# The state-space stage's two ends: scales and statistics across the stage border, and the order of the last outputs and turns

## The chip, the cores and the metric

The kernel runs on one core of a Trainium2 chip. Its engines are TensorE (PE; PEld is its weight load), VectorE (DVE), ScalarE (ACT), GpSimd (POOL) and SyncE (SP, which here issues DMAs). Each executes its own list of instructions in order; they meet only at semaphores. The metric is the device time of one execution in microseconds (us), lower is better; the time of a kernel is the median of several executions.

## The reference, cut to what matters

The input `x` is 16 batches of 512 rows with 128 elements. Four blocks follow one another, each with a residual:

```
x = x + attn_a(layernorm(x))      # attention with a Gaussian kernel, 16 heads
x = x + ffn(layernorm(x))         # local attention, and attention over routed tokens
x = x + attn_b(layernorm(x))      # the state-space block
x = x + ffn(layernorm(x))         # the same ffn again
```

The state-space block, on batches of 1024 rows in the original and of 512 here, is

```
u = h * rsqrt(mean(h*h) + 1e-6) * norm_weight     # h = layernorm(x)
Bu = u @ B_bar.T                                  # complex, 32 states
xs = scan over the rows of each batch: s = Lam_bar * s + Bu
y = 2 * (re(xs) @ C_re.T - im(xs) @ C_im.T) + D * u
out = h + y                                       # and x = x + out
```

The ffn behind it starts with two norms of its input and with router scores, the products of the normalised rows with two routing tokens.

## The kernel before, in words

`x` stays in SBUF the whole time as 64 tiles of 128 rows by 128 elements, four tiles to a batch, eight to a pair of batches. The stages are the Gaussian attention, the ffn's local part (`stage_light`, tag f1), its routed part (`stage_heavy`, tag f1), the state-space stage (`stage_ssm`), and the ffn again with tag f2. Every stage is a block: all engines finish it before any engine starts the next. Inside a block the order of each engine is written out by hand and the engines wait for counts of semaphores. In these sections a stage's pairs are numbered 0 to 7.

**The routed stage**, `stage_heavy` (L1669), loops over n with steps of pair n, n-1 and n-2 interleaved. For the last pair (n = 8 and 9) there remain, on ACT, the exponentials, `turned(7)` (L1952, two copies out of PSUM, L1956) and `values(7)` (L1959); on PE `turn`, `values`, `output` and `scatter` (L1889); on DVE `places` (L2063), `nulls` (L2079), `heavy(7)` (L2085) and `residual(7)` (L2091, which adds the result to `x`). Behind each residual comes `statistics` (L2094): `bn_stats` of each of the pair's eight tiles and `bn_aggr`, giving mean and variance in `K["mv"]`. ACT's last instruction is a load of the table for square roots (L1988), which comes ahead of the stage that uses it.

**The state-space stage**, `stage_ssm` (L2142), starts with a chain on DVE over all 64 tiles (L2221 to L2233, each step waits for the one before): add 1e-5 to the variance, root (ACT, L2316), reciprocal, two products, add 1e-6, a second root (ACT, L2320), reciprocal, products. It yields four columns per tile: `a1`, `a0` (scale and bias of the doubly normalised row) and `h1`, `h0` (for x + layernorm(x)). PE turns the matrix `bb` (L2394) and ACT copies it (L2318). Then, per pair q:

- `rows(q)` on ACT (L2327) makes eight normalised tiles `un`; of pairs 0 and 1 ACT makes four tiles and DVE four (L2237).
- `turn(q)` on PE (L2403) transposes them into the two banks `tp`, and `leave(q)` on ACT (L2333) copies them out as `ut`.
- `inputs(q)` on PE (L2413), `rotate(q)` on DVE (L2244), a sum on POOL (L2388), `scan(q)` on DVE (L2249), `back(q)` on DVE (L2254).
- `outputs(q)` on PE (L2424, L2429) into the banks `yy`; it waits for `back(q)` and for DVE's `residual(q-1)`, which frees `yy`.
- `kept(q)` on POOL (L2380) puts h into `x`; `residual(q)` on DVE (L2261) adds `yy`; then `statistics(q)` (L2266, L2270), `root(q)` on ACT (L2337), `scales(q)` on DVE (L2277).
- `result(q)` on ACT (L2348) makes the normalised rows `y` of the next stage; of pair 7 it makes four tiles, DVE the other four (L2298).
- `turn_result(q, e)` on PE (L2440) transposes each half e of the pair into the one bank `ty`, `leave_result(q, e)` on ACT (L2342) copies it to `yt`, and `score(b)` on PE (L2446) multiplies it with the routing tokens into `srow`. At the very end DVE makes the columns `r2` and `rc` for the next stage with one more root (`two`, L2359), and ACT copies `srow` (L2370).

PE's loop (L2449) goes over p from -3 to 10 and in each round does `inputs(p+1)`, `turn_result(p-2, 0)`, `turn(p+2)`, `turn_result(p-2, 1)`, `outputs(p)` and, in odd rounds from 3 on, four scores. ACT's loop (L2352) has `rows(p+3)`, `leave_result(p-2, 0)`, `leave(p+2)`, `root(p-1)`, `leave_result(p-2, 1)`, `result(p-1)`. So the outputs of the last pair (p = 7) stand behind both turns of pair 5, and with one bank `ty` every turn waits for the copy of the turn before.

## Time and profile before

| | us |
|---|---|
| median of 3 runs | 1805.41 (1804.49 to 1809.51) |
| the profiled execution: its time | 1804.04 |
| the profiled execution: its span | 1802.2 |
| state-space stage in that span | 1084.6 to about 1185.3 |

The span runs from the first to the last instruction that the profiler recorded; the execution's time has some 2 us around it. The profile's mean granted clock of TensorE is 0.977 of full speed. In a timeline each row is one instruction, or several alike merged (x8), with its start, its length, the engine and the line, what it writes from what it reads, and in brackets how long the engine had been idle and whose instruction ended the wait. Ends of PE's matmuls are modelled, and merged matmuls overlap.

### The profile page before, as it was taken

To read this page: it belongs to the slowest core of one execution; us is meant where nothing else is said; L and a number is where in the kernel's file an instruction comes from. 1 tells how busy PE (TensorE), PEld (TensorE's weight loads), DVE (VectorE), ACT (ScalarE), POOL (GpSimd) and SP (SyncE) were. 2 spreads that over 40 slices of the span, in tenths; PEclk is the share of its full clock that TensorE was granted. 3 is DMA by queue.
4 is the path that set the end of the run, shared out by engine and by line. 5 is a ranking of instruction groups with operands and counts; after the bars stand their busy time and mean duration, and the time that the engine had idled before them with its cause. 6 is when DMAs were issued, how large, how long until landed. Compare 5 with 4: busy or idle time off the path is not lost. (4 is left out here: it accounts for less than half of the span.)

```text
span 1802.2 us, 68292 instructions
## 1 busy us (share of the span) xinstructions
PE 1646.6 (91%) x27609; PEld 1271.0 (71%) x27609; DVE 1458.1 (81%) x3482; ACT 1454.3 (81%) x4122; POOL 759.2 (42%) x853
## 2 busy tenths in 40 slices
PE   3888988898899999999997996879999999999897
PEld 1444444444588888888886874658888888888786
DVE  8999999999877777877898776747777777789775
ACT  4999999998788888888774666668888888877564
POOL 2010000001154554555446966425454545554795
PEclk7999999999999999999999998989999999999998
DMA  6656555552001010101012000000101010101211
GB/s 189 152 150 156 144 138 141 147 131 55 13 15 26 15 26 15 26 15 26 14 27 49 2 1 1 1 13 15 26 15 26 14 26 15 26 14 27 49 49 48
DMA packets 80041, 91.96 MB, mean 51 GB/s; under 512 B 11696, under 2 KB 67984, under 8 KB 79728
## 3 DMA queue, kind: packets, MB, share of 16 engines
q1 hardware_dynamic: 78432, 87.15, 19.3%
q8 instruction: 221, 3.62, 0.9%
q14 instruction: 92, 0.75, 0.1%
q10 hardware_dynamic: 1296, 0.44, 0.1%
HBM read 39.68 MB, written 31.10 MB: 39 GB/s over the span
## 5 line engine op out<-in xcount | busy, mean ns | idle before, releaser
L1633 POOL TENSOR_TENSOR f1l_pn<-f1l_p,f1l_rs 128x512 f32<-128x512 f32 (+1 forms) x256 | 206.3, 827 | 252.5 <-DVE f1l_rs L1326 250.4
L1633 POOL TENSOR_TENSOR f2l_pn<-f2l_p,f2l_rs 128x512 f32<-128x512 f32 (+1 forms) x256 | 206.2, 826 | 231.1 <-DVE f2l_rs L1326 231.1
L1205 ACT ACTIVATE f2l_p<-f2l_sm,f2l_nb 128x192 f32<-128x192 f32 x512 | 209.2, 435 | 43.0 <-DVE f2l_nb L1319 43.0
L1205 ACT ACTIVATE f1l_p<-f1l_sm,f1l_nb 128x192 f32<-128x192 f32 x512 | 209.4, 434 | 42.4 <-DVE f1l_nb L1319 37.8
L595 ACT ACTIVATE r_pr<-r_far 128x1536 f32<-128x1536 f32 x128 | 194.2, 1517 | 0.1
L432 PE MATMUL r_acc<-r_pr,r_vp 128*32 128x384 f32 x3528 | 189.6, 331 | 2.2 <-DVE r_pr L709 1.2
L698 DVE SCALAR_TENSOR_TENSOR r_pr<-r_pr,k_lo,r_cap 128x512 f32<-128x512 f32 x256 | 182.3, 752 | 10.4 <-ACT r_pr L595 10.0
L709 DVE TENSOR_SCALAR r_pr<-r_pr,k_hi,k_lo 128x768 f32<-128x768 f32 x256 | 164.1, 682 | 0.0
L595 ACT ACTIVATE r_pr<-r_near 128x1024 f32<-128x1024 f32 x128 | 138.4, 1082 | 2.8 <-PE r_near L403 2.8
L1319 DVE TENSOR_REDUCE f2l_nb<-f2l_sm 128x4 f32<-128x768 f32 x128 | 116.1, 948 | 15.8 <-PE f2l_sm L1019 15.8
L775 POOL TENSOR_TENSOR r_nw<-r_nv,r_nr 128x8 f32<-128x8 f32 x1 | 0.4, 356 | 295.1 <-ACT r_nr L570 295.1
L1319 DVE TENSOR_REDUCE f1l_nb<-f1l_sm 128x4 f32<-128x768 f32 x128 | 116.1, 948 | 8.4 <-PE f1l_sm L1019 8.3
L432 PEld LDWEIGHTS r_acc<-r_pr,r_vp 128*32 128x32 f32 x3528 | 85.8, 110 | 42.2 <-issue 29.6
L1342 DVE TENSOR_TENSOR f2l_ot<-f2l_xa,f2l_late 128x256 f32<-128x256 f32 x128 | 53.7, 419 | 75.7 <-ACT f2l_late L1197 75.7
L1205 ACT ACTIVATION_READ_ACCUMULATOR f2l_p<-f2l_sm,f2l_nb 128x1 f32 x512 | 113.0, 221 | 0.0
L1205 ACT ACTIVATION_READ_ACCUMULATOR f1l_p<-f1l_sm,f1l_nb 128x1 f32 x512 | 112.6, 220 | 0.0
L1332 DVE COPY f1l_pt<-f1l_tp 128x512 f32<-128x512 f32 x128 | 88.1, 688 | 21.8 <-PE f1l_tp L1038 18.9
L1332 DVE COPY f2l_pt<-f2l_tp 128x512 f32<-128x512 f32 x128 | 88.0, 688 | 18.7 <-PE f2l_tp L1038 15.4
L1342 DVE TENSOR_TENSOR f1l_ot<-f1l_xa,f1l_late 128x256 f32<-128x256 f32 x128 | 53.6, 419 | 61.0 <-ACT f1l_late L1197 60.8
L1019 PE MATMUL f2l_sm<-f2l_kt,f2l_qt 64*64 64x128 f32 (+1 forms) x3584 | 99.3, 248 | 0.4 <-ACT f2l_p L1205 0.4
L1019 PE MATMUL f1l_sm<-f1l_kt,f1l_qt 64*64 64x128 f32 (+1 forms) x3584 | 99.1, 248 | 0.0
L1019 PEld LDWEIGHTS f2l_sm<-f2l_kt,f2l_qt 64*64 64x64 f32 x3584 | 92.9, 134 | 0.8 <-ACT f2l_p L1205 0.6
(564 smaller groups left out, 5155.7 us busy)
## 6 DMA issues: line engine op xcount, KB each, us to landing
rbf_rows<-r_part SPq DMA_DIRECT2D x112, 128.0 KB, 2.1
r_qs<-rbf_rows SPq DMA_DIRECT2D x60, 192.0 KB
r_ks<-rbf_rows SPq DMA_DIRECT2D x60, 192.0 KB
f1l_vs<-f1l_vv SPq DMA_DIRECT2D x64, 128.0 KB, 2.5
f2l_vs<-f2l_vv SPq DMA_DIRECT2D x64, 128.0 KB, 2.4
rbf_rows<-r_part SPq DMA_DIRECT2D x16, 384.0 KB, 3.0
rbf_rows<-r_part SPq DMA_DIRECT2D x16, 256.0 KB, 3.0
out<-k_x SPq DMA_DIRECT2D x8, 512.0 KB, 3.2
```

What stands on the lines that cost most here:

```text
L432: mm = nc.tensor.matmul(acc[32 * g:32 * g + 32, q0:q0 + n], vp[:, par, t, g, 32 * q:32 * q + 32], pr[:, (PAIRS * b + 2 * q + g // 2) % RIN ...
L595: nc.scalar.activation(pr[:, n % RING, :, cols], src, ACT.Exp).then_inc(done, 1)
L698: ins = nc.vector.scalar_tensor_tensor(on, on, K["lo"][:, h:h + 1], cap[:, h, :].unsqueeze(1).broadcast_to([P, NT, P]), ALU.max, ALU.min)
L709: ins = nc.vector.tensor_scalar(off, off, hi, lo, ALU.min, ALU.max)
L775: nc.gpsimd.tensor_tensor(nw[:], nv[:], nr[:], ALU.mult).then_inc(s_nv, 1)
L1019: mm = nc.tensor.matmul(sm[64 * w:64 * w + 64, u % 2, e, cc * PW + P * side:cc * PW + P * side + kn], qt[r, par, c, at:at + W], kt[r, par, ...
L1205: ins = nc.scalar.activation(p[:, u % 2, k, :], sm[:, u % 2, k // 2, k % 2 * PW:(k % 2 + 1) * PW], ACT.Exp, bias=nb[:, u % 2, k:k + 1], ac ...
L1319: nc.vector.tensor_reduce(nb[:, u % 2, :], sm[:, u % 2, :, 0:2 * PW].rearrange("p a (k c) -> p a k c", k=2), AX, ALU.max, negate=True).the ...
L1332: nc.vector.tensor_copy(pt[:, u % 2, 0:HU * P], tp[:]).then_inc(s_pt, 1)
L1342: nc.vector.tensor_tensor(ot[:, u // 2 % 2, 2 * g:2 * g + 2, :], xa[:, 0, 0:2 * P].rearrange("p (c q) -> p c q", q=P), late[:, u % 2, :].r ...
L1633: ins = nc.gpsimd.tensor_tensor(pn[:, u % 2, at:at + HU * w].rearrange("p (k c) -> p k c", k=HU), p[:, u % 2, :, cols], r.broadcast_to([P, ...
```

## The change

Four things are done.

- The scales of pairs 0 to 6 (56 tiles) are made at the end of the f1 routed stage: `scales_begin` on DVE behind `nulls(7)`, `scales_end` on DVE between `heavy(7)` and `residual(7)`, their two roots on ACT as its last instructions. The load of the table for roots comes ahead of `turned(7)` for that. `a1`, `a0`, `h1`, `h0` become tensors that outlive the stage.
- The statistics of pair 7 leave the routed stage; the state-space stage makes them, and pair 7's scales, on DVE between its rows of pairs 0 and 1 and the first `rotate`. Their two roots stand in ACT's order behind `leave(0)` and behind `rows(2)`. `rows(7)` and `kept(7)` wait for them.
- `outputs(7)` comes ahead of the turns of pair 5, and the last part of PE's and ACT's order is written out.
- From pair 5 on, the turns of the second half of a pair go to the first bank of `tp`, which is free behind the last `leave`; the others go to `ty`. So a turn waits for the copy of the last but one.

The diff, without its declarations of tensors and the renamed counts of waits:

```diff
@@ stage_heavy, ACT
+                if n == M and stats:
+                    nc.scalar.preload_act_table_set("sqrt_and_others")
...
             if stats:
-                nc.scalar.preload_act_table_set("sqrt_and_others")
+                act.wait_ge(v_s, 2 * (M - 1) + 1)
+                nc.scalar.activation(K["rstd"][:, KNOWN], K["rstd"][:, KNOWN], ACT.Sqrt).then_inc(a_s, 1)
+                act.wait_ge(v_s, 2 * (M - 1) + 5)
+                nc.scalar.activation(r3[:], r3[:], ACT.Sqrt).then_inc(a_s, 1)
@@ stage_heavy, DVE
+            link = Chain(dve, v_s)
+            link.n = 2 * (M - 1)
+            rstd, mean, var = K["rstd"][:, KNOWN], K["mv"][:, KNOWN, 0], K["mv"][:, KNOWN, 1]
+            def scales_begin():
+                dve.wait_ge(v_s, 2 * (M - 1))
+                link(nc.vector.tensor_scalar(rstd, var, 1e-5, None, ALU.add))
+                nc.vector.tensor_scalar(nm[:], mean, -1.0, None, ALU.mult)
+                dve.wait_ge(a_s, 1)
+                link(nc.vector.reciprocal(rstd, rstd))
+                link(nc.vector.tensor_tensor(vy[:], var, rstd, ALU.mult))
+                link(nc.vector.tensor_tensor(vy[:], vy[:], rstd, ALU.mult))
+                link(nc.vector.tensor_scalar(r3[:], vy[:], 1e-6, None, ALU.add))
+            def scales_end():
+                nc.vector.tensor_tensor(K["h0"][:, KNOWN], nm[:], rstd, ALU.mult)
+                link(nc.vector.tensor_scalar(K["h1"][:, KNOWN], rstd, 1.0, None, ALU.add))
+                dve.wait_ge(a_s, 2)
+                link(nc.vector.reciprocal(r3[:], r3[:]))
+                nc.vector.tensor_tensor(K["a1"][:, KNOWN], rstd, r3[:], ALU.mult)
+                link(nc.vector.tensor_tensor(K["a0"][:, KNOWN], K["h0"][:, KNOWN], r3[:], ALU.mult))
...
                 if n >= 2:
                     heavy(n - 2)
+                if n == M + 1 and stats:
+                    scales_end()
...
-                if n >= 2 and stats:
+                if 2 <= n <= M and stats:
                     statistics(n - 2)
                 if 1 <= n <= M:
                     places(n - 1)
                     nulls(n - 1)
+                if n == M and stats:
+                    scales_begin()
@@ stage_ssm
+        LATE = N - 3
+        def turned(q, e):
+            return tp[:, 0, :] if q >= LATE and e else ty[:]
@@ stage_ssm, DVE (the chain over 64 tiles goes; behind the rows of pairs 0 and 1:)
+            last = tiles(N - 1)
+            rstd, mean, var = K["rstd"][:, last], K["mv"][:, last, 0], K["mv"][:, last, 1]
+            for j in range(2 * NT):
+                ins = v.bn_stats(st6[:, j, :], K["x"][:, last.start + j, :])
+            ins.then_inc(s_st, 1)
+            dve.wait_ge(s_st, 1)
+            for j in range(2 * NT):
+                ins = v.bn_aggr(K["mv"][:, last.start + j, :], st6[:, j, :])
+            ins.then_inc(s_st, 1)
+            dve.wait_ge(s_st, 2)
+            link(v.tensor_scalar(rstd, var, 1e-5, None, ALU.add))
...
+            link(v.tensor_tensor(a0[:, last], h0[:, last], r3[:], ALU.mult))
@@ stage_ssm, ACT
             def rows(q):
                 wait(act, s_t, q - 1)
+                if q == N - 1:
+                    act.wait_ge(s_d, 8)
...
-            for p in range(-AFTER, N + AFTER):
+            for p in range(-AFTER, N - 1):
                 if 0 <= p + 3 < N:
                     rows(p + 3)
+                if p + 3 == 2:
+                    last_second_root()
...
                 if 0 <= p + 2 < N:
                     leave(p + 2)
+                if p + 2 == 0:
+                    last_root()
...
+            root(N - 2)
+            result(N - 2)
+            leave_result(N - 3, 0)
+            leave_result(N - 3, 1)
+            root(N - 1)
+            leave_result(N - 2, 0)
+            result(N - 1)
+            leave_result(N - 2, 1)
+            leave_result(N - 1, 0)
+            act.wait_ge(s_d, 12)
+            a(two[:], two[:], ACT.Sqrt).then_inc(s_a, 1)
+            leave_result(N - 1, 1)
@@ stage_ssm, PE
+                if q >= LATE and e:
+                    pe.wait_ge(s_te, N)
+                wait(pe, s_ye, 2 * q + e - (q > LATE or q == LATE and e == 1))
...
-            for p in range(-AFTER, N + AFTER):
+            for p in range(-AFTER, N - 1):
...
+            outputs(N - 1)
+            for q in (N - 3, N - 2):
+                turn_result(q, 0)
+                turn_result(q, 1)
+                score(2 * q - 2)
+                score(2 * q - 1)
+            turn_result(N - 1, 0)
+            turn_result(N - 1, 1)
+            for b in range(B - RG, B):
+                score(b)
```

## Rows read from the trace of the kernel before

**Rows 1.** The page: busy time (share of the span) and instructions of each engine

```profile
PE 1646.6 (91%) x27609; PEld 1271.0 (71%) x27609; DVE 1458.1 (81%) x3482; ACT 1454.3 (81%) x4122; POOL 759.2 (42%) x853
```

**Rows 2.** Timeline of DVE: start us, length us, engine, line, operation, [idle before <- releaser]

```profile
1079.18 0.29 DVE L2085 TENSOR_TENSOR f1h_hv<-f1h_ps,k_null_q 128x128 f32<-128x128 f32 x1 [1.91 <-PE f1h_ps L1878]
1080.74 1.22 DVE L2091 TENSOR_TENSOR k_x<-k_x,f1h_ps 128x1024 f32<-128x1024 f32 x1 [1.26 <-PE f1h_ps L1889]
...
1084.63 0.20 DVE L2221 TENSOR_SCALAR k_rstd<-k_mv 128x64 f32<-128x64 f32 x1 [0.32 <-PEq L2138]
...
1086.48 0.23 DVE L2228 TENSOR_TENSOR s_h<-s_nm,k_rstd 128x64 f32<-128x64 f32 x1
...
1087.83 2.14 DVE L2237 TENSOR_SCALAR s_un<-k_x,s_a 128x128 f32<-128x128 f32 x8
1096.49 0.69 DVE L2244 TENSOR_TENSOR s_t<-s_xx,k_c_cc 128x512 f32<-128x512 f32 x1 [6.52 <-PE s_xx L2413]
```

**Rows 3.** Timeline of ACT, end of the routed stage and start of the state-space stage

```profile
1073.85 0.60 ACT L1956 ACTIVATE f1h_pt<-f1h_ps 128x512 f32<-128x512 f32 x1 [0.95 <-PE f1h_ps L1854]
1075.03 0.60 ACT L1956 ACTIVATE f1h_pt<-f1h_ps 128x512 f32<-128x512 f32 x1 [0.58 <-PE f1h_ps L1854]
...
1085.11 0.28 ACT L2318 ACTIVATE s_bbt<-s_xx 128x128 f32<-128x128 f32 x1
...
1087.83 3.19 ACT L2327 ACTIVATE s_un<-k_x,s_a 128x128 f32<-128x128 f32 x8 [1.09 <-DVE s_a L2233]
1091.54 1.11 ACT L2333 ACTIVATE s_ut<-s_tp,k_norm_w 128x1024 f32<-128x1024 f32 x1 [0.52 <-PE s_tp L2403]
```

**Rows 4.** Timeline of PE: a turn, outputs of pairs 6 and 7, last turns, scores

```profile
1121.68 0.66 PE L2440 MATMUL s_ty<-k_ident,f_y 128*128 128x128 f32 x4 [2.04 <-ACT s_yt L2342]
...
1157.50 2.06 PE L2424 MATMUL s_yy<-k_c_g,s_v 64*128 64x128 f32 x32
1159.49 2.05 PE L2429 MATMUL s_yy<-k_c_dd,s_ut 128*128 128x128 f32 x16
...
1166.57 3.79 PE L2424 MATMUL s_yy<-k_c_g,s_v 64*128 64x128 f32 x32
...
1179.07 1.12 PE L2440 MATMUL s_ty<-k_ident,f_y 128*128 128x128 f32 x4 [3.31 <-ACT f_y L2348]
...
1181.98 2.67 PE L2446 MATMUL s_srow<-s_yt,k_rtz 128*32 128x512 f32 x8
```

**Rows 5.** Timeline of DVE: residuals of pairs 6 and 7

```profile
1161.95 1.21 DVE L2261 TENSOR_TENSOR k_x<-k_x,s_yy 128x1024 f32<-128x1024 f32 x1
...
1172.88 1.22 DVE L2261 TENSOR_TENSOR k_x<-k_x,s_yy 128x1024 f32<-128x1024 f32 x1 [6.48 <-PE s_yy L2429]
```

**Rows 6.** Two stretches: busy PE, PEld, DVE, ACT, POOL; granted clock, DMA share, GB/s

```profile
1092.80:1096.40 3.60, 3.60 (x9) 0.85 (x9) 0.00 (x0) 2.92 (x8) 0.34 (x1) 0.52 0.00 0
1166.50:1172.80 6.30, 6.30 (x53) 5.89 (x53) 0.00 (x0) 3.67 (x9) 0.00 (x0) 0.61 0.00 0
```

**Rows 7.** Timeline of ACT, end of the state-space stage

```profile
1167.16 3.17 ACT L2348 ACTIVATE f_y<-k_x,s_y,k_rstd 128x128 f32<-128x128 f32 x8
...
1177.37 1.65 ACT L2348 ACTIVATE f_y<-k_x,s_y,k_rstd 128x128 f32<-128x128 f32 x4
1180.22 0.60 ACT L2342 ACTIVATE s_yt<-s_ty 128x512 f32<-128x512 f32 x1 [1.21 <-PE s_ty L2440]
1180.72 0.30 ACT L2359 ACTIVATE s_two<-s_two 128x128 f32<-128x128 f32 x1
...
1184.69 0.60 ACT L2370 ACTIVATE k_srow<-s_srow 128x512 f32<-128x512 f32 x1 [2.00 <-PE s_srow L2446]
```

**Rows 8.** Timeline of ACT at the kernel's start: a table load and what follows

```profile
5.16 1.28 ACT L514 ACT_TABLE_LOAD   x1 [5.16 <-issue]
6.45 0.20 ACT L514 ACTIVATE r_rstd<-r_rstd 128x4 f32<-128x4 f32 x1
```

**Rows 9.** The scores' line: ns min/median/max, first and last start

```profile
L2446 PE MATMUL s_srow<-s_yt,k_rtz x32: 592/617/1064, 1134.6 to 1183.6; 128*32 128x512 f32 x32
```

More of the change, by code:

```diff
@@ L1705, in stage_heavy @@
         st6 = sb("st6", [P, 2 * NT, 6])
+        if stats:
+            vy, r3, nm = (sb(n, [P, 2 * NT * (M - 1)]) for n in ("vy", "r3", "nm"))
         W_ = ctx.enter_context(nc.psum_tensor(tag + "h_ps", [P, 8, BANK], F32))
@@ L1745, in stage_heavy @@
         s_out = sem("out")
+        a_s = sem("as")
         SCALE = float(DH) ** -0.5
+        KNOWN = slice(0, 2 * NT * (M - 1))
         work = ctx.enter_context(ExitStack())
@@ L2155, in stage_ssm @@
         vy = sb("vy", [P, T])
-        r3 = sb("r3", [P, T])
-        nm = sb("nm", [P, T])
-        a1 = sb("a1", [P, T])
-        a0 = sb("a0", [P, T])
-        h1 = sb("h1", [P, T])
-        h0 = sb("h0", [P, T])
+        r3 = sb("r3", [P, 2 * NT])
+        nm = sb("nm", [P, 2 * NT])
+        a1, a0, h1, h0 = (K[n] for n in ("a1", "a0", "h1", "h0"))
         y0 = sb("y0", [P, T])
@@ L2239, in _ @@
                 ins.then_inc(s_unv, 1)
+            last = tiles(N - 1)
[9 more added lines that the diff above has]
+            link(v.tensor_scalar(rstd, var, 1e-5, None, ALU.add))
+            v.tensor_scalar(nm[:], mean, -1.0, None, ALU.mult)
+            dve.wait_ge(s_a, 1)
+            link(v.reciprocal(rstd, rstd))
+            link(v.tensor_tensor(vy[:, last], var, rstd, ALU.mult))
+            link(v.tensor_tensor(vy[:, last], vy[:, last], rstd, ALU.mult))
+            link(v.tensor_scalar(r3[:], vy[:, last], 1e-6, None, ALU.add))
+            v.tensor_tensor(h0[:, last], nm[:], rstd, ALU.mult)
+            link(v.tensor_scalar(h1[:, last], rstd, 1.0, None, ALU.add))
+            dve.wait_ge(s_a, 2)
+            link(v.reciprocal(r3[:], r3[:]))
+            v.tensor_tensor(a1[:, last], rstd, r3[:], ALU.mult)
+            link(v.tensor_tensor(a0[:, last], h0[:, last], r3[:], ALU.mult))
+            assert link.n == 8
             def rotate(q):
@@ L2267, in statistics @@
                 ins.then_inc(s_st, 1)
-                dve.wait_ge(s_st, 2 * q + 1)
+                dve.wait_ge(s_st, 2 * q + 3)
                 for j in range(2 * NT):
@@ L2314, in _, with last_root, last_second_root @@
             a = nc.scalar.activation
-            act.wait_ge(s_d, 1)
-            a(K["rstd"][:], K["rstd"][:], ACT.Sqrt).then_inc(s_a, 1)
+            last = tiles(N - 1)
+            def last_root():
+                act.wait_ge(s_d, 1)
+                a(K["rstd"][:, last], K["rstd"][:, last], ACT.Sqrt).then_inc(s_a, 1)
+            def last_second_root():
+                act.wait_ge(s_d, 5)
+                a(r3[:], r3[:], ACT.Sqrt).then_inc(s_a, 1)
             act.wait_ge(s_b, 1)
             a(bbt[:], xx[:, 0, 0:P], ACT.Copy).then_inc(s_bt, 1)
-            act.wait_ge(s_d, 5)
-            a(r3[:], r3[:], ACT.Sqrt).then_inc(s_a, 1)
-            act.wait_ge(s_d, 8)
             def rows(q):
                 wait(act, s_t, q - 1)
+                if q == N - 1:
+                    act.wait_ge(s_d, 8)
                 for j in range(NT if q < SHARED else 2 * NT):
@@ L2341, in leave_result @@
                 wait(act, s_sc, 2 * q + e - RG + 1)
-                a(yt[:, (2 * q + e) % RG], ty[:], ACT.Copy).then_inc(s_ye, 1)
+                a(yt[:, (2 * q + e) % RG], turned(q, e), ACT.Copy).then_inc(s_ye, 1)
             def result(q):
@@ L2350, in result @@
                 ins.then_inc(s_ny, 1)
-            for p in range(-AFTER, N + AFTER):
+            for p in range(-AFTER, N - 1):
                 if 0 <= p + 3 < N:
                     rows(p + 3)
+                if p + 3 == 2:
+                    last_second_root()
                 if 0 <= p - 2 < N:
                     leave_result(p - 2, 0)
-                if p - 2 == N - 1:
-                    act.wait_ge(s_d, 12)
-                    a(two[:], two[:], ACT.Sqrt).then_inc(s_a, 1)
                 if 0 <= p + 2 < N:
                     leave(p + 2)
+                if p + 2 == 0:
+                    last_root()
                 if 0 <= p - 1 < N:
@@ L2377, in kept @@
                     pool.wait_ge(s_unv, q + 1)
+                if q == N - 1:
+                    pool.wait_ge(s_d, 8)
                 for j in range(2 * NT):
@@ L2437, in turn_result @@
                     pe.wait_ge(s_nyv, 1)
-                wait(pe, s_ye, 2 * q + e)
+                if q >= LATE and e:
+                    pe.wait_ge(s_te, N)
+                wait(pe, s_ye, 2 * q + e - (q > LATE or q == LATE and e == 1))
                 for j in range(NT):
-                    mm = nc.tensor.transpose(ty[:, j * P:(j + 1) * P], K["y"][:, NT * (2 * q + e) + j, :], K["ident"][:])
+                    mm = nc.tensor.transpose(turned(q, e)[:, j * P:(j + 1) * P], K["y"][:, NT * (2 * q + e) + j, :], K["ident"][:])
                 mm.then_inc(s_yt, 1)
@@ L2493, in program @@
             load(n, A[n], [P, E])
-        for n in ("rstd", "r2", "rc"):
+        for n in ("rstd", "r2", "rc", "a1", "a0", "h1", "h0"):
             K[n] = sb(n, [P, T])
```

16 lines of the change are left out of this document (1 added, 15 removed).

## The prediction

> **What bounds the kernel now.** I read the page first: over the span TensorE (PE) is busy 91%, VectorE (DVE) and ScalarE (ACT) 81% each [rows 1]. That average says little, since the change touches only the two ends of one stage, the state-space stage, some 102 us of 1802. So I read the timelines of DVE, ACT and PE round its start and its end, to see what each first and last instruction waited for.
>
> At the start, DVE is alone on the path: after the last residual of the routed stage (1080.74, 1.22 us) it takes the last pair's statistics until 0.32 us before 1084.63, where the next stage opens, then a chain of small operations on all 64 tiles up to 1087.83, and only then can normalised rows be made [rows 2]. ACT makes its first rows at 1087.83 as well [rows 3], and DVE then idles 6.52 us for PE [rows 2]. At the end PE gets the last pair's outputs at 1166.57, behind the turns of pair 5, though their inputs and their bank had been ready since DVE's residual of pair 6 ended at 1163.16 [rows 4, 5]. They run at 0.61 of the clock [rows 6], DVE waits 6.48 us for them [rows 5], and after them come statistics, the last outputs, turns, copies and scores, one after another, up to the copy of the scores at 1184.69 [rows 7]. Both ends are drained pipelines, so what is saved there is saved whole: the stage behind starts when this one is finished.
>
> **The start, step by step.** Three things go from the path.
>
> (a) Statistics of the last pair leave the routed stage. Its DVE then ends with the residual, at 1081.96 instead of 0.32 before 1084.63, that is 1084.31: 2.35 us. PE, ACT and GpSimd are finished by then. The next stage opens at 1082.28.
>
> (b) The scales of pairs 0 to 6 move into DVE's idle time there. Their first half (add, negate, root, reciprocal, two products, add) takes 1086.48 - 1084.63 = 1.85 us at a width of 64, the second half 1087.83 - 1086.48 = 1.35 [rows 2]; 56 wide they are no longer. The first half goes in front of `heavy`, where DVE idles 1.91 us, the second in front of the last residual, where it idles 1.26 [rows 2]. 1.85 of 1.91 fits; 1.35 against 1.26 is 0.1 too much, which I count as 0 to 0.1 since the narrower reciprocal is shorter. Behind the waiting DVE stand only `heavy` and the residual, which PE's scatter and this stage's end wait for; if the cover were gone they would be late by up to 1.3 to 1.9.
>
> (c) The square-root table load moves up behind the last exponentials. ACT idles 0.95 us before its copy at 1073.85, so it is free at 1072.90; a load takes 1.28 us [rows 8] and ends at 1074.18. The first copy is 0.33 late and ends at 1074.78, the second starts at 1075.03 as before [rows 3]. Cost nothing. One rule speaks against the change. In the trace the instruction behind a load starts 0.01 us after it [rows 8]. The Trainium skill, "ScalarE: Activation LUTs", section "What ACT_TABLE_LOAD costs", states a load of about 1.28 us plus a drain of about 1.38; the load's length agrees, the drain does not show. By the Trainium skill both copies would be late and the stage's end with them, an estimate of 1.1 us less gain, 11.6.
>
> In the new stage ACT's first rows need the turned input matrix: its copy starts 0.48 after the stage opens and takes 0.28 [rows 3]. So rows start at 1082.28 + 0.76 = 1083.04 instead of 1087.83, 4.79 earlier. From there to the copy of the first turned pair took 3.71 (1087.83 to 1091.54), so that copy is at 1086.75 and ends 1.11 later; PE's inputs fill 1092.80 to 1096.45 at a granted clock of 0.52 [rows 6], 3.65, and end at about 1091.66. Meanwhile DVE makes its eight rows (2.14 us) until 1084.4, the moved statistics (1081.96 to 1084.31 before, 2.35) until 1086.8, and a chain of the same two halves, now 8 wide, so at most 1.85 and 1.35. In it stand two roots of ACT, and ACT executes in its own order: the first behind the copy that ends at 1087.86, the second behind the eight rows of pair 2, 3.2 us more [rows 3], so at 1091.3. The rest of the chain, a short reciprocal and two products, leaves DVE free at 1091.9. `rotate(0)`, queued behind it, was at 1096.49 [rows 2] and comes at 1091.9 rather than 1091.66. **Gain of the start: 4.6 us.** ACT's two small roots fall into waits of the filling pipeline. The added waits for the last pair's scales (ACT's rows and GpSimd's kept tokens of pair 7) come long after the scales are ready. No DMA is issued, moved or passed; the new semaphore adds one clear to SP's at a stage's start, when SP has nothing else to do. From `rotate(0)` the order of all engines is as before up to pair 5, so the shift is carried along whole.
>
> **The end, step by step.** Clock times here are those of before; the shift of the start comes on top. Outputs of pair 7 start behind the residual of pair 6, at 1163.3 instead of 1166.57. At the full clock outputs take 4.05 (1157.50 to 1159.49 + 2.05 [rows 4]) where they took 6.3. They end at 1167.4 and DVE's last residual starts there instead of at 1172.88: 5.5 earlier. From that residual to ACT's last outputs is 4.49 (1172.88 to 1177.37 [rows 5, 7]), so they start at 1171.87 and take 1.65, to 1173.5. What had been between has to fit beside it. ACT's outputs of pair 6 now come before the copies of pair 5, at 1166.5 to 1169.6 (3.17 for eight tiles [rows 7]), the two copies of pair 5 follow to 1170.6, PE turns pair 6 at 1170.2 and 1170.8 into two banks, and ACT copies its first half at 1171.3, behind the root, just ahead of its last outputs. The slack is some 0.5 us.
>
> Then the tail, which was from 1179.07, the first turn of pair 7, to 1184.69, with turns of 1.1 and four scores in 2.67 at half clock [rows 4, 7]. With two banks: turn 1173.6 to 1174.2 (0.66 at the full clock [rows 4]), the other right behind it at 1174.05 to 1174.7, no longer waiting for the copy of the first. Copy of the first 1174.25 to 1174.85 (0.60), root of `two` 0.30, copy of the second 1174.95 to 1175.55. Only one score is left behind it, two matmuls of 0.59 each at the full clock and 1.06 at the low one [rows 9], overlapping a little: about 1.05. The copy of the scores starts at 1176.65 instead of 1184.69. DVE's last reciprocals, fed by the root, end before it does. **Gain of the end: 8.05 us.**
>
> **Sum.** 4.6 + 8.05 = 12.65. The profiled execution had a span of 1802.2 and a time of 1804.04, so 1791.4; that execution lies 1.4 below the median of 1805.41, and from the median it is 1792.8. Not shown in the trace is the clock that PE will be granted. At the start bounds are 0 (inputs of pair 0 were at the low clock already) and, if the low stretch lasts into pair 1, 1 to 2 us lost. Outputs of pair 7: 4.05 or 6.3. I take the full clock, since the nearest row is the turn at 1121.68, at full speed behind 2.04 us of idleness [rows 4], and the pause here is 1.7. Last turns and score: 8.05 becomes 6.4 at the low clock. The next stage's first projections can meet either clock; half of a stretch of 3 us, near the first one's length [rows 6], is 1.5 us to either side, an estimate.
>
> **Rivals.**
> (1) *The clock stays low at the end.* The turn at 1179.07 took 1.12 behind 3.31 us of idleness, that at 1121.68 only 0.66 [rows 4]. PE is idle here 1.7, 1.3 and 1.65 us with work between, so a fall is possible. Outputs slow: 2.2 less; tail slow: 1.65 less; with one of them or both the gain is about 10, 1795.4. Chance 0.20.
> (2) *The table load holds ACT longer than its row.* If it held it once more for its own length, 1.28 us [rows 8], ACT would be free at 1075.46, the second copy would end at 1076.66 instead of 1075.63, and PE, `heavy` and the last residual would be 1.0 late: gain 11.6, 1793.8. It is the drain of the Trainium skill that would do this. Against it stands the instruction 0.01 us behind a load [rows 8]. Chance 0.05.
> (3) *The start gives little more than the statistics.* DVE's first half overruns `heavy`, or `rotate(0)` waits longer for the second root, queued behind eight rows of ACT: a wait in place of the chain. Start gain 2.35 to 3.5, sum about 11, 1794.5. Chance 0.08.
> (4) *ACT's new order binds at the end.* With 0.5 us of slack, the copy of pair 6 may push the last outputs; with a low clock at both ends besides, the sum falls to 4 or 5, 1801, inside 0.3%. Chance 0.05.
> (5) *Slower.* At half clock each microsecond loses half a microsecond of PE's work. If the earlier start lets the clock stay low from the first inputs on, while the stage fills (1088 to 1123), the 12.65 are paid back after some 25 us; at 35 us low the kernel is slower by 5, 1810. Against it: the dense outputs of pair 7 got the full clock back within their 6.3 us, since their mean was 0.61 and not 0.50 [rows 6]. Chance 0.03.
> That the change does nothing is excluded by the idle times in DVE's rows [rows 2, 5], in which the moved work stood on the chain.
>
> **How the numbers follow.** The forecast has the remaining 0.59, with 1792.8. The range starts at all favourable: warmer first projections and a start of 4.9 make 14.5, 1790.9, less 1.4 for a draw like the profiled one, 1789.5. It ends at rivals 1 and 3 together with slow first projections: 12.65 - 3.85 - 1 - 1.5 is 6.3, 1799. 0.3% is 5.4 us, about what a measurement of this kernel can tell from no change. Forecast and rivals 1 to 3 are 0.92, of which 0.01 may fall inside: faster 0.91, same 0.06, slower 0.03.
>
> **What would show it.** Right: no statistics of eight tiles after the last residual of the routed stage; the state-space stage's first rows 0.8 us after it opens; `rotate(0)` 4.6 nearer to the last residual; outputs of pair 7 directly behind the residual of pair 6 with a granted clock of 1.00; the last residual 5.5 nearer to it; turns of pair 7 0.5 apart. Wrong: `heavy` later than 1079.2, an ACT gap behind the table load, outputs of 6 us, or copies of pair 6 after the last outputs' inputs are ready.

## The result and the profile after

The changed kernel took 1794.84 us (median of 4 runs, 1793.89 to 1799.18) against 1805.39 for the kernel before (4 runs, 1804.49 to 1809.51): ratio 0.9946, 95% interval [0.9929, 0.9962], so faster by 7 to 13 us. The prediction had 1792.8 in a range of 1789.5 to 1799.0, and "faster". The profiled execution took 1795.58 with a span of 1793.8.

The page of the kernel after, its first part, answers to [rows 1] and shows almost the same busy times, a few instructions more on DVE and ACT: no engine works less, the ends are shorter.

```profile
PE 1643.5 (92%) x27609; PEld 1267.5 (71%) x27609; DVE 1461.3 (81%) x3493; ACT 1455.3 (81%) x4124; POOL 760.2 (42%) x853
```

**The start.** Timeline of DVE after (start, length, engine, line, operation, [idle before <- releaser]), the rows that answer to [rows 2]:

```profile
1081.39 0.19 DVE L2125 TENSOR_SCALAR f1h_r<-f1h_vy 128x56 f32<-128x56 f32 x1
1081.89 0.29 DVE L2094 TENSOR_TENSOR f1h_hv<-f1h_ps,k_null_q 128x128 f32<-128x128 f32 x1 [0.31 <-PE f1h_ps L1882]
...
1083.12 0.21 DVE L2133 TENSOR_TENSOR k_a<-k_h,f1h_r 128x56 f32<-128x56 f32 x1
1083.50 1.22 DVE L2100 TENSOR_TENSOR k_x<-k_x,f1h_ps 128x1024 f32<-128x1024 f32 x1 [0.18 <-DVE k_a L2133]
1085.05 2.14 DVE L2259 TENSOR_SCALAR s_un<-k_x,k_a 128x128 f32<-128x128 f32 x8 [0.32 <-PEq L2173]
...
1093.60 0.20 DVE L2283 RECIPROCAL s_r<-s_r 128x8 f32<-128x8 f32 x1 [2.08 <-ACT s_r L2370]
...
1094.16 0.69 DVE L2291 TENSOR_TENSOR s_t<-s_xx,k_c_cc 128x512 f32<-128x512 f32 x1
```

The last residual of the routed stage is now the last thing DVE does there: the stage behind opens 0.32 after it ends, and rows are made at once. `rotate(0)` (the last row) comes 10.66 us behind that residual (1094.16 - 1083.50) where it came 15.75 behind it (1096.49 - 1080.74 [rows 2]): 5.1 less. The chain of the last pair ends at 1094.08 and PE's inputs end at 1094.05, so neither waits for the other.

**The table load and the filling.** Timelines of ACT and of PE after, the rows that answer to [rows 3]:

```profile
1075.57 1.28 ACT L1983 ACT_TABLE_LOAD   x1
1076.86 0.60 ACT L1960 ACTIVATE f1h_pt<-f1h_ps 128x512 f32<-128x512 f32 x1
1077.69 0.60 ACT L1960 ACTIVATE f1h_pt<-f1h_ps 128x512 f32<-128x512 f32 x1 [0.23 <-PE f1h_ps L1858]
...
1085.38 0.28 ACT L2373 ACTIVATE s_bbt<-s_xx 128x128 f32<-128x128 f32 x1 [3.52 <-PE s_xx L2464]
1085.56 3.18 ACT L2381 ACTIVATE s_un<-k_x,k_a 128x128 f32<-128x128 f32 x8
1089.11 1.11 ACT L2387 ACTIVATE s_ut<-s_tp,k_norm_w 128x1024 f32<-128x1024 f32 x1 [0.37 <-PE s_tp L2473]
```

```profile
1085.05 0.30 PE L2464 MATMUL s_xx<-k_ident,k_c_bb 128*128 128x128 f32 x1 [1.65 <-PEq L2173]
1087.25 1.82 PE L2473 MATMUL s_tp<-k_ident,s_un 128*128 128x128 f32 x8 [1.90 <-ACT s_un L2381]
1090.37 3.68 PE L2483 MATMUL s_xx<-s_ut,s_bbt 128*64 128x512 f32 x8 [1.30 <-ACT s_ut L2387]
```

The copy behind the load starts 0.01 us after it, and the second copy still waits for PE (0.23): the load is hidden, as it was costed. PE's first inputs run at half clock as before (3.68).

**The end.** Timelines of PE, DVE and ACT after, the rows that answer to [rows 4, 5, 7]:

```profile
1161.06 2.06 PE L2494 MATMUL s_yy<-k_c_g,s_v 64*128 64x128 f32 x32 [1.77 <-DVE k_x L2308]
1163.04 2.05 PE L2499 MATMUL s_yy<-k_c_dd,s_ut 128*128 128x128 f32 x16
...
1171.34 0.66 PE L2512 MATMUL s_ty<-k_ident,f_y 128*128 128x128 f32 x4 [1.23 <-ACT f_y L2402]
1171.90 0.63 PE L2512 MATMUL s_tp<-k_ident,f_y 128*128 128x128 f32 x4
1172.46 1.94 PE L2518 MATMUL s_srow<-s_yt,k_rtz 128*32 128x512 f32 x8
```

```profile
1159.70 1.22 DVE L2308 TENSOR_TENSOR k_x<-k_x,s_yy 128x1024 f32<-128x1024 f32 x1
...
1165.13 1.22 DVE L2308 TENSOR_TENSOR k_x<-k_x,s_yy 128x1024 f32<-128x1024 f32 x1 [0.97 <-PE s_yy L2499]
```

```profile
1168.95 0.21 ACT L2391 ACTIVATE k_rstd<-k_rstd 128x8 f32<-128x8 f32 x1 [0.60 <-DVE k_rstd L2320]
1169.07 0.58 ACT L2396 ACTIVATE s_yt<-s_ty 128x512 f32<-128x512 f32 x1
1169.63 1.65 ACT L2402 ACTIVATE f_y<-k_x,s_y,k_rstd 128x128 f32<-128x128 f32 x4
...
1174.44 0.60 ACT L2438 ACTIVATE k_srow<-s_srow 128x512 f32<-128x512 f32 x1 [1.14 <-PE s_srow L2518]
```

Outputs of pair 7 start 0.14 behind the end of the residual of pair 6, and the two residuals are 5.43 apart instead of 10.93. The turns of pair 7 are 0.56 apart, the second no longer behind the copy of the first. ACT's new order leaves it 0.60 idle before the last root. The windows of these stretches after (columns as in [rows 6]: length, busy PE, PEld, DVE, ACT, POOL, granted clock, DMA share, GB/s) give half clock for the inputs and the full clock for outputs, turns and scores:

```profile
1090.40:1094.00 3.60, 3.60 (x9) 0.82 (x9) 1.34 (x9) 3.10 (x9) 0.42 (x1) 0.50 0.00 0
1161.10:1165.10 4.00, 4.00 (x50) 3.88 (x51) 2.68 (x19) 1.81 (x6) 0.00 (x0) 1.00 0.00 0
1171.40:1174.40 3.00, 3.00 (x16) 1.20 (x16) 1.57 (x5) 1.64 (x4) 0.00 (x0) 1.00 0.00 0
```

### The profile page after: what moved, and what is told of

The parts are those of the page before. It is cut to its first block and busy times, and to the rows that moved or that the text cites. A ratio compares the mean times of both kernels' runs of the same rounds, so it can differ in the third digit from the quotient of the medians.

```text
span 1793.8 us, 68313 instructions
## 1 busy us (share of the span) xinstructions
PE 1643.5 (92%) x27609; PEld 1267.5 (71%) x27609; DVE 1461.3 (81%) x3493; ACT 1455.3 (81%) x4124; POOL 760.2 (42%) x853
```

## The experiments

All were compared with the kernel before on the same chip: *alloc_only* to *again* on one, *outputs_back* to *load_back* on a second, *late_half* to *warm_all* on a third. There is one profile of each. Beside the ratios I use one table, in us, read from DVE's and ACT's timelines of each profile: *residual* and *rotate(0)*, counted from `heavy` of pair 6 in the routed stage; *middle*, from `rotate(0)` to the residual of pair 6; *outputs*, from there to the residual of pair 7; *tail*, from there to the copy of the scores; *next*, from there to the first reduction over scores of the local stage behind; and their *total* from `heavy` of pair 6.

```
kernel            residual rotate(0) middle outputs  tail   next   total   ratio to before
before                9.35    25.10  65.46  10.93  11.81  12.17  125.47
after                 9.45    20.11  65.54   5.43   9.31  12.62  113.01   0.9946 [0.9929, 0.9962]
alloc_only            9.34    25.13  69.19   8.16  11.35  13.37  127.20   1.0001 [0.9993, 1.0010]
start_only            9.45    20.25  69.14   8.16  11.35  13.36  122.26   0.9976 [0.9968, 0.9985]
end_only              9.34    25.13  69.07   5.44   9.31  12.11  121.06   0.9963 [0.9950, 0.9975]
again                 9.45    20.25  69.14   5.44   9.31  12.15  116.29   0.9930 [0.9917, 0.9943]
outputs_back         10.37    21.31  65.53   8.84   9.31  13.19  118.18   0.9949 [0.9930, 0.9969]
one_bank              9.45    20.39  65.54   5.43  11.61  12.07  115.04   0.9926 [0.9905, 0.9948]
statistics_back       9.46    22.75  65.55   5.44   9.31  13.34  116.39   0.9946 [0.9928, 0.9964]
load_back            10.10    21.04  65.53   5.44   9.30  12.63  113.94   0.9932 [0.9908, 0.9956]
late_half            10.37    21.31  65.59   5.44   9.30  12.63  114.27   0.9943 [0.9920, 0.9965]
warm_fill             9.46    20.16  65.54   5.43   9.30  12.63  113.06   0.9932 [0.9915, 0.9950]
warm_start            9.46    17.87  65.59   5.44   9.31  12.63  110.84   0.9925 [0.9909, 0.9941]
warm_all              9.45    17.87  65.58   5.44   9.31  11.43  109.63   0.9919 [0.9903, 0.9934]
```

### The two halves of the change

**Only the tensors allocated.** The kernel before, with the change's four tensors of scales kept beside the others and not used: does the new place of things in memory matter?

```diff
-        for n in ("rstd", "r2", "rc"):
+        for n in ("rstd", "r2", "rc", "a1", "a0", "h1", "h0"):
```

> The kernel before, with only the four columns a1, a0, h1, h0 made tensors that outlive the stages (unused there); it shifts the addresses of all later tensors by 1 KB per partition. The profiled change saved 12.5 us between the routed stage's last pairs and the next stage's first scores, but 8.4 us of the span: the unchanged local stages f1 and f2 took 2.5 and 1.1 us longer. If that is variation between executions, this kernel is the same as before, 0 to 2 us either way, and its local stages in the profile take whatever they take. If the new addresses cost it, it is 2 to 4 us slower than before (ratio 1.001 to 1.002) and the profile shows f1's local stage at 497 us rather than 494.5.

Ratio 1.0001 [0.9993, 1.0010]: it does not, since 2 us would be 1.0011. The sign in the profile misled: the first local stage took 497.2 us here too, but 494.3 in *outputs_back* and 494.5 in *late_half*, which have the same tensors. This profile did show two things of the old order that the first one had not, both of them clock: a middle of 69.19 us instead of 65.46, and outputs of pair 7 at full clock (2.06 for the first half instead of 3.79 [rows 4]).

**Only the start, only the end, both again.** The start alone is the change with PE's and ACT's old loops and one bank of turns (both edits cut to their main lines):

```diff
-            for p in range(-AFTER, N - 1):
+            for p in range(-AFTER, N + AFTER):
...
-            outputs(N - 1)
-            for q in (N - 3, N - 2):
...
@@ turned
-            return tp[:, 0, :] if q >= LATE and e else ty[:]
+            return ty[:]
```

> The change with the end of the state-space stage as before (outputs of the last pair behind pair 5's turns, one bank). Theory: both ends are drained pipelines and add up: 4.6 to 5.0 us faster than before, ratio 0.9973; rotate(0) about 13.4 us behind the start of the routed stage's last residual step instead of 15.75. Rival, that an early start is given back in the filling stage or at its end: 0 to 2 us.

The end alone is the reverse: the kernel before, with the change's loop ends and second bank.

```diff
-            for p in range(-AFTER, N + AFTER):
+            for p in range(-AFTER, N - 1):
...
+            outputs(N - 1)
+            for q in (N - 3, N - 2):
...
@@ turned
+            return tp[:, 0, :] if q >= LATE and e else ty[:]
```

> The kernel before with only the end of the state-space stage changed. Theory: 7.9 to 8.1 us faster than before when the last outputs get the full clock (ratio 0.9955), 4.5 to 6.5 when the clock falls there; from the residual of pair 6 to the copy of the scores 14.8 us instead of 22.7. Rival, that the two parts need one another: under 6 with the full clock.

The third is the changed kernel itself, unedited.

> The changed kernel once more, beside the others on one chip: the sum of start_only and end_only, 12 to 13 us faster than before by the theory (ratio 0.9930); 10 to 11 if the missing 2 us are real, as by new addresses.

With a median of 1806.31 for the kernel before, the ratios are 4.3 us for the start (interval 2.7 to 5.8), 6.7 for the end (4.5 to 9.0) and 12.6 for both (10.3 to 15.0). 4.3 + 6.7 = 11.0, inside the last interval. In the table, these four profiles share a middle of 69.1, so they compare well: alloc_only to start_only is 4.94, alloc_only to end_only 6.14, to both 10.91. So the parts add up, and neither pays the other back.

Two of the expectations were wrong in a number. That of *start_only* has `rotate(0)` 13.4 behind the last residual, which is 15.75 less the statistics alone; it came 10.80 behind it (20.25 - 9.45). That of *end_only* has 7.9 to 8.1 us if the last outputs get the full clock. They got it (5.44), and from the residual of pair 6 to the copy of the scores it took the 14.8 us expected, but the old order had the full clock as well here: it took 19.51 (8.16 + 11.35) and not 22.74 (10.93 + 11.81), so the end is worth 4.8 us in the stage. The other 1.3 of the 6.14 are the next stage's first projections (13.37 against 12.11), whose low stretch was shorter. The 8 us come only when the old order catches the low clock: 2.8 of them in the turns of pair 5 and the outputs of pair 7, 0.5 in the first turn of pair 7 (1.12 [rows 4] against 0.66).

### The end, piece by piece

**Outputs of pair 7 back behind the turns of pair 5.**

```diff
-            outputs(N - 1)
             for q in (N - 3, N - 2):
                 turn_result(q, 0)
                 turn_result(q, 1)
+                if q == N - 3:
+                    outputs(N - 1)
```

> The change with one line moved: PE's outputs of the last pair stand behind the two turns of pair 5 again; second bank, ACT's order and the start stay. Theory: between the residuals of pairs 6 and 7 DVE now has 5.44 us; here the outputs wait for ACT's outputs of pair 5 and two turns, so it is at least 1.6 us longer, 7.1 to 8.2, and up to 10.9 if the clock falls in front of them: 2 to 4 us slower than the change (ratio to before 0.994 to 0.995). Rival, that the second bank had made the early outputs needless: under 0.5 us longer.

Timeline of PE in this kernel:

```profile
1160.73 0.66 PE L2512 MATMUL s_ty<-k_ident,f_y 128*128 128x128 f32 x4 [2.57 <-ACT f_y L2402]
1161.22 0.60 PE L2512 MATMUL s_tp<-k_ident,f_y 128*128 128x128 f32 x4
1161.75 3.65 PE L2494 MATMUL s_yy<-k_c_g,s_v 64*128 64x128 f32 x32
1165.33 2.05 PE L2499 MATMUL s_yy<-k_c_dd,s_ut 128*128 128x128 f32 x16
```

Its window over the first half of the outputs (columns as above):

```profile
1161.70:1165.30 3.60, 3.60 (x34) 3.46 (x32) 0.99 (x10) 2.44 (x7) 0.00 (x0) 0.53 0.00 0
```

PE waits 2.57 instead of 1.77, does the turns first, and the first half of the outputs takes 3.65 at half clock: residual 7 is 3.4 later. Of that, 1.6 is the clock (3.65 - 2.06) and 1.8 the place in the order (1.6 at least was expected). The ratio, 0.9949 against 0.9926 to 0.9946 of the others on this chip, points the same way, but its interval [0.9930, 0.9969] doesn't separate it from all of them.

**One bank for the turns.**

```diff
-                if q >= LATE and e:
-                    pe.wait_ge(s_te, N)
-                wait(pe, s_ye, 2 * q + e - (q > LATE or q == LATE and e == 1))
+                wait(pe, s_ye, 2 * q + e)
...
-            return tp[:, 0, :] if q >= LATE and e else ty[:]
+            return ty[:]
```

> The change with one bank for all turns of results. Theory: the second turn of pair 7 waits for the copy of the first half, which costs the tail a copy and its two handovers, 0.7 to 1.2 us: from the last residual to the copy of the scores 10.0 to 10.5 us instead of 9.31. Pair 6's turns have slack and cost nothing. Rival, that ACT's order sets the tail: no difference (9.3).

The tail is 11.61 instead of 9.31, 2.3 us and not the 0.7 to 1.2 expected, because pair 6's turns had no slack. Timelines of ACT and PE in this kernel:

```profile
1167.27 0.60 ACT L2396 ACTIVATE s_yt<-s_ty 128x512 f32<-128x512 f32 x1 [0.75 <-PE s_ty L2510]
...
1168.83 0.60 ACT L2396 ACTIVATE s_yt<-s_ty 128x512 f32<-128x512 f32 x1 [0.88 <-PE s_ty L2510]
1169.33 1.64 ACT L2402 ACTIVATE f_y<-k_x,s_y,k_rstd 128x128 f32<-128x128 f32 x4
...
1175.40 0.60 ACT L2438 ACTIVATE k_srow<-s_srow 128x512 f32<-128x512 f32 x1 [1.14 <-PE s_srow L2516]
```

```profile
1171.59 0.63 PE L2510 MATMUL s_ty<-k_ident,f_y 128*128 128x128 f32 x4 [0.47 <-ACT s_yt L2396]
1173.00 0.63 PE L2510 MATMUL s_ty<-k_ident,f_y 128*128 128x128 f32 x4 [0.78 <-ACT s_yt L2396]
```

The second bank works in two places. The last turns are 1.41 apart instead of 0.56: from the start of the last outputs to the copy of the scores it takes 6.07 (1175.40 - 1169.33) instead of 4.81 (1174.44 - 1169.63), 1.26. And ACT waits for turns ahead of its last outputs (0.75 and 0.88), so these start 5.54 behind residual 7 (at 1163.79 here) instead of 4.50: 1.04, what the new order of ACT would cost with one bank (rival 4). In the time of the whole kernel 2.3 us are 0.13%, and the ratio doesn't show them.

### The start, piece by piece

**Statistics back in the routed stage.** The last pair's statistics are made behind the last residual again; the scales stay as changed.

```diff
@@ stage_heavy, DVE
-                if 2 <= n <= M and stats:
+                if n >= 2 and stats:
...
@@ stage_ssm, DVE
-            for j in range(2 * NT):
-                ins = v.bn_stats(st6[:, j, :], K["x"][:, last.start + j, :])
...
```

> The change with the last pair's statistics in the routed stage again; its scales stay in the state-space stage. Theory: the stage opens 2.35 us later and rotate(0) comes 22.4 to 22.6 us behind the heavy step of pair 6 instead of 20.1 to 20.25, so the other half of the start's gain (2.6 of 4.9 us) is that of the chain over 56 tiles. Rival, that rotate(0) is set by DVE's chain in the new stage and its two roots: under 1 us later, since the statistics leave that chain.

`rotate(0)` is 2.64 later, and the total 3.4, with 0.7 of it in *next*. Of the 2.64 the statistics are 2.35, as forecast, and the rest is clock. From the last residual to `rotate(0)` it takes 13.29 us here (22.75 - 9.46) and 10.94 in *one_bank* (20.39 - 9.45), which has the change's start: 2.35 apart. In the profile after it takes 10.66, because PE's turn of the input matrix took 0.30 there and that of the first pair 1.82; here and in *one_bank* they took 0.45 and 1.97. The first of these in *one_bank*:

```profile
1083.42 0.45 PE L2464 MATMUL s_xx<-k_ident,k_c_bb 128*128 128x128 f32 x1 [1.64 <-PEq L2173]
```

So at the clock of the kernel before the start is worth 4.7 us (25.10 - 20.39): 2.35 the statistics, 2.36 the wide chain. The last pair's own chain does not care: its root queues behind ACT's rows instead.

**Table load back.**

```diff
-                if n == M and stats:
-                    nc.scalar.preload_act_table_set("sqrt_and_others")
...
+                nc.scalar.preload_act_table_set("sqrt_and_others")
                 act.wait_ge(v_s, 2 * (M - 1) + 1)
```

> The change with the load of the square-root table behind ACT's last copy again, in front of the first root. Theory: the root starts 0.9 to 1.0 us later, heavy of pair 7 comes 8.7 to 8.8 us behind that of pair 6 instead of 7.84, and the end of the stage with it: 1 us slower than the change. Rival, that the load with a drain is longer than its row: 2.3 us or more, and then ACT's copies would have shown it in the change too.

Timelines of ACT and of DVE in this kernel:

```profile
1081.00 1.28 ACT L1992 ACT_TABLE_LOAD   x1
1082.30 0.25 ACT L1994 ACTIVATE k_rstd<-k_rstd 128x56 f32<-128x56 f32 x1
```

```profile
1082.58 0.50 DVE L2121 RECIPROCAL k_rstd<-k_rstd 128x56 f32<-128x56 f32 x1 [1.01 <-ACT k_rstd L1994]
...
1083.85 0.29 DVE L2093 TENSOR_TENSOR f1h_hv<-f1h_ps,k_null_q 128x128 f32<-128x128 f32 x1
```

The load lies on the path of the first root here, `heavy` has no idle time ahead of it any more, and the residual is 0.65 late (10.10), where 0.9 to 1.0 was expected. `rotate(0)` comes 0.93 later than after, but 10.94 behind the residual as in *one_bank*, so 0.28 of that is the clock of the two turns again. So moving the load up is worth 0.65 us. The root starts 0.02 behind the load, and the load itself starts 0.01 behind the copy ahead of it: no drain shows where one would have been on the path.

**The last pair's second half behind `rotate(0)`.** Does `rotate(0)` wait for the chain in front of it?

```diff
-            dve.wait_ge(s_a, 2)
-            link(v.reciprocal(r3[:], r3[:]))
...
+                if p + 1 == 0:
+                    last_end()
```

> The change with the second half of the last pair's scales (a reciprocal and two products) behind rotate(0) on DVE, into the wait for GpSimd's sum. Theory: rotate(0) started 0.1 us behind the end of PE's inputs already, so it comes 0.1 us earlier at the low clock and the rest stays: same as the change within 0.3 us. Rival, that DVE's chain holds the start: 0.5 us or more faster.

This profile has the routed stage's last scatter at half clock (2.08 instead of 1.16), as that of outputs_back has, whose start is the changed kernel's; so these two are compared: 10.94 from the last residual to `rotate(0)` in both. The chain costs nothing there; PE's inputs end no sooner. The scatter's clock costs 0.92 at the residual and nothing behind it: 10.94 is also what *one_bank* and *load_back* show, whose scatters had the full clock.

### The clock

**Idle transposes in the middle.** In four of the ten profiles told of so far, late_half aside (alloc_only, start_only, end_only, again), the clock fell in the middle of the stage. (The expectation below says eight profiles; ten is right.) These four are all the profiles of the first chip, and none of those of the other two chips shows the fall; for before and after the chip is not on record. Timeline of PE in *again*, with two of its low stretches, and its windows (columns as above):

```profile
1113.81 0.66 PE L2512 MATMUL s_ty<-k_ident,f_y 128*128 128x128 f32 x4 [2.45 <-ACT f_y L2402]
1114.30 1.29 PE L2473 MATMUL s_tp<-k_ident,s_un 128*128 128x128 f32 x8
1117.37 1.11 PE L2512 MATMUL s_ty<-k_ident,f_y 128*128 128x128 f32 x4 [1.78 <-ACT s_yt L2396]
1118.41 3.64 PE L2494 MATMUL s_yy<-k_c_g,s_v 64*128 64x128 f32 x32
...
1138.12 0.66 PE L2512 MATMUL s_ty<-k_ident,f_y 128*128 128x128 f32 x4 [1.99 <-ACT s_yt L2396]
1138.71 3.69 PE L2494 MATMUL s_yy<-k_c_g,s_v 64*128 64x128 f32 x32
```

```profile
1114.00:1122.00 8.00, 6.22 (x49) 5.37 (x48) 5.41 (x23) 7.89 (x20) 6.67 (x9) 0.57 0.00 0
1138.00:1142.50 4.50, 4.38 (x37) 4.00 (x38) 3.23 (x10) 4.02 (x11) 4.50 (x7) 0.62 0.01 2
```

The turn between the two waits took 1.29 us here (1.30, 1.41 and 1.50 in the other three) instead of 1.04 in the kernel after, and its granted clock was 0.75 instead of 1.00, so the clock fell during it, ahead of the second wait. The experiment fills both waits, those of round p = 2 of the changed kernel, with transposes of the identity into banks that are free there; nothing reads them.

```diff
+                if p == 2:
+                    for _ in range(18):
+                        nc.tensor.transpose(ty[:, 0:P], K["ident"][:], K["ident"][:])
                 if 0 <= p - 2 < N:
                     turn_result(p - 2, 0)
...
+                if p == 2:
+                    for _ in range(14):
+                        nc.tensor.transpose(srow[:, 0:P], K["ident"][:], K["ident"][:])
```

> The change with 18 idle transposes on PE ahead of the first turn of results of pair 0 and 14 ahead of the second, in waits of 2.5 and 2.0 us, into banks that are not in use. In four of the eight profiles of the twelve-run series so far (before, the change and six variants) PE's clock fell in the middle of the stage and the residual of pair 6 came 69.1 us behind rotate(0), in the others 65.5. Theory: these two waits are what lets the clock fall; filled, every profile shows 65.4 to 65.7 and no low stretch between 1100 and 1160, and the median is 1 to 2.5 us below the change. Rival, that the fall has another cause or that the filling delays PE: the same, or up to 1 us slower.

Its middle is 65.54. But so were those of the other six of the ten, without filling, after among them with the same waits (2.49 and 2.03), and that of late_half, on the same chip as this one. Where the fall showed the filling was not run, so this profile can't show that it prevents the fall, and the ratio, 0.9932 [0.9915, 0.9950], isn't better than that of *again*. Inconclusive.

**Idle transposes at the start.** On top of late_half, 8 behind the last scatter of the routed stage and 15 behind the turn of the input matrix.

```diff
+            if stats:
+                for _ in range(8):
+                    nc.tensor.transpose(W_[:, KB, 0:P], K["ident"][:], K["ident"][:])
...
+            for _ in range(15):
+                nc.tensor.transpose(xx[:, 1, 0:P], K["ident"][:], K["ident"][:])
```

> late_half with 8 idle transposes on PE at the end of the routed stage and 15 behind the turn of the input matrix. Theory: the clock stays full over the border, the first turn takes 1.1 and the first inputs 1.94 us instead of 1.8 and 3.7; rotate(0) comes 17.5 to 18 us behind the heavy step of pair 6 instead of 20.1 to 20.25, 2 us faster than late_half. Rival, that the pause at the border alone lets it fall: no gain, and the first turn up to 1 us later.

Timeline of PE in this kernel:

```profile
1083.89 1.80 PE L2472 MATMUL s_xx<-k_ident 128*128 128x128 f32 x15
1085.96 1.09 PE L2481 MATMUL s_tp<-k_ident,s_un 128*128 128x128 f32 x8 [0.26 <-ACT s_un L2387]
1088.59 1.94 PE L2491 MATMUL s_xx<-s_ut,s_bbt 128*64 128x512 f32 x8 [1.54 <-ACT s_ut L2393]
```

The first turn takes 1.09 instead of 1.82 and the inputs 1.94 instead of 3.68, and `rotate(0)` comes 2.24 sooner (17.87, inside the 17.5 to 18 expected). The granted clock over both rows is 1.00, where it was 0.50 over late_half's first turn. The low clock at the start is a price of PE's idleness, and idle work that delays nothing takes it away. Here late_half's edit is needed: ACT's second root for the last pair starts at 1091.61, behind `rotate(0)` at 1090.63. In the ratio, 0.9925 [0.9909, 0.9941] against late_half's 0.9943 [0.9920, 0.9965], the gain doesn't show clear of noise.

**All three, and the next stage's first projections.** Both fillings, with 14 and 10 transposes round the local stage's first turn.

```diff
+                for _ in range(14):
+                    nc.tensor.transpose(sm[:, 0, 0, 0:P], K["ident"][:], K["ident"][:])
                 turn_x(0)
+                for _ in range(10):
+                    nc.tensor.transpose(sm[:, 0, 0, 0:P], K["ident"][:], K["ident"][:])
```

> warm_start and warm_fill together, and in the next local stage 14 idle transposes ahead of its first turn and 10 behind it. Theory: 2 us from the start, 1 to 2.5 from the filling stage, 1 to 2 from the first projections, 4 to 6 us faster than the change (ratio to before 0.990 to 0.991) and a narrower spread. Rival, that the clock is not what these ends wait for: within 1 us of the change (0.993).

Timeline of PE here, in the local stage's first projections; the same operation at the like place took 0.63 in the kernel after (1180.86):

```profile
1176.23 0.40 PE L972 MATMUL f2l_xa<-k_xh,k_wqkv_h 128*128 128x512 f32 x1
1176.47 0.39 PE L975 MATMUL f2l_xa<-k_xl,k_wqkv_h 128*128 128x512 f32 x1
```

*Next* is 11.43 instead of 12.62, and the total 3.4 us less than after. At 0.9919 [0.9903, 0.9934] this kernel has the lowest ratio of all; against *again*, 0.9930 [0.9917, 0.9943] from another comparison, the intervals overlap, so it is not shown to be faster than the change, and 3.4 us are 0.19%, less than these intervals can tell. The 4 to 6 us and the narrower spread that were expected did not show: its six times span 6.5 us, the five of *again* 3.7. Part of what spreads the times goes with the clock: in *warm_fill*, 1792.04 us had a mean granted clock of 0.986 and 1801.61 one of 0.978.

## Why the prediction was right, and where it was off

**Statistics leave the routed stage (a): right.** 2.35 expected, 2.35 when put back, at equal clock.

**The scales of pairs 0 to 6 in the idle time (b): right.** The first half fits, with 0.31 of idle time left before `heavy`. The residual is 0.10 later behind `heavy` of pair 6 than before, as counted at most; the row names the chain's last product as its releaser.

**Table load (c) and rival 2: right, rival 2 didn't come.** The next instruction starts 0.01 and 0.02 us behind a load in the two kernels above. By the Trainium skill, "ScalarE: Activation LUTs", section "What ACT_TABLE_LOAD costs", a drain of some 1.38 us would follow; with it the gain would have been 11.6. The load's own length agrees with the trace (1.28), the drain doesn't, and the measurement decides.

**The start's sum, 4.6: 5.0 measured** (25.10 - 20.11). The copy of the input matrix came 0.33 behind the opening instead of 0.48, since PE's turn ran at full clock (0.30), and the first turned pair followed 3.55 behind ACT's rows instead of 3.71. These 0.3 are the clock of one execution: in *one_bank*, whose start is the same, both turns were at the low clock, and there the gain is 4.7. The forecast of a tie between the chain and PE's inputs (0.24 apart) held: 0.03 apart. Rival 3 fell.

**The end's sum, 8.05: 8.0 measured**, 5.50 at the residual (10.93 - 5.43) and 2.50 in the tail (11.81 - 9.31), with ACT's slack of 0.60 where 0.5 was worked out. Outputs and turns had the full clock, so rivals 1 and 4 fell in this execution. One step was incomplete: the sum took the old end from one profile as if it had one duration. Its outputs of pair 7 at 6.3 us are one of two. In alloc_only and start_only, which have the old order at the end, they were at full clock, and there the end is worth 4.8 in the stage, not 8 (2.72 at the residual, 2.04 in the tail). The bound 4.05 or 6.3 was on the list for the changed kernel only. That 8.0 came out as forecast rests on comparing with the very profile from which it was worked out.

**"The shift is carried along whole": right for the order, incomplete for the clock.** The middle was 65.46 before and 65.54 after; but in four profiles, of old and new orders alike, it was 3.6 longer because of the low stretches shown above. What decides whether they come is open: all four are profiles of one chip, and *again* is the very kernel whose profile after had none. So the chip, or what went with that series of runs, stands as a rival to chance, and no run here parts the two. The slower rival (5), a low clock while the stage fills, thus names something that exists, but it comes without the change as well (alloc_only, end_only), at 3.6 us.

**From the 13 us of the ends to the time.** The total of the table fell by 12.46: 4.99 + 8.00, less 0.08 in the middle and 0.45 of slower first projections (12.62 against 12.17). The span fell by 8.4 only. The rest lies in stages that the change doesn't touch: from the first to the last score matmul of the two local stages it took 494.5 and 478.2 us before, 496.9 and 479.3 after, and over the fourteen profiles these lengths go from 494.3 to 497.2 and from 478.2 to 481.1, without an order that any edit explains. In another comparison, with 23 runs of the kernel before, *again* gave 12.6 us. That this meets the forecast's 12.65 to the tenth is luck: its interval is 10.3 to 15.0, and its profile against alloc_only's has 10.9. That the first median missed by 2 us is within what such stages vary; it was not traced further.

## What to carry to other kernels

Where two stages meet, every engine but one drains: small operations on the narrow path there (scales, statistics, a table load) can often go into idle time that the timeline shows a few microseconds earlier, and each term can be read off the trace to a few tenths, as long as the clock is the same on both sides. Put the last long matmul group in front of short turns that only feed later work, and give alternating turns a second bank when an engine must copy them in a fixed order. Before claiming a few microseconds of a kernel of 1800, look at whether the row on which the claim rests has one duration or two, by the clock that was granted.

## What was not expected of the hardware

TensorE's clock differs between executions of the same code at the same place: the first half of an outputs group took 2.06 or 3.64 us (2.4 and 1.2 GHz by the windows' clock of 1.00 and 0.53), behind a first wait of nearly the same length (2.49 at full clock in *after*, 2.45 with the fall in *again*). Those two may come from different chips; the routed stage's last scatter took 1.16 or 2.08 on one chip, in *one_bank* and *outputs_back*, whose code is the same up to there. Idle transposes in the first waits of the stage took both turn and inputs to the full clock in the two profiles that had them (1.82 to 1.09, 3.68 to 1.94). And unchanged stages of 494 us differ by up to 2.9 us from one execution to the next, which is more than most of the edits here are worth.
